# Moving x's transposes behind P times V, and splitting tile 1's normalisation between VectorE and GpSimd, in a five-phase attention kernel

## The reference

```
def _attn(xq, xc, Wq, Wk, Wv, Wo, bo):          # 16 heads of 64
    q, k, v = xq @ Wq, xc @ Wk, xc @ Wv
    attn = softmax(q k^T * 64 ** -0.5)
    return (attn v) @ Wo + bo
x = _attn(_ln(x, g1, b1), _ln(x, g1, b1), ...1) + x      # SELF
x = _attn(_ln(x, g2, b2), context, ...2) + x             # CROSS
x = _geglu_ff(_ln(x, g3, b3), Wp, bp, Wf, bf) + x        # GEGLU
out = attention of 16 heads of 8 over the context        # CROSS2
return x + out + ffn(_ln(out, ln_g, ln_b))               # FFN
```

## Time and profile before

| | |
|---|---|
| median of 3 runs | 451.22 us (450.65 to 452.02) |
| the profiled execution | 450.97 us, span 449.3 us |
| granted TensorE clock | 1.0 of full speed in all 40 slices |
| PE busy | 434.4 us, 97% of the span |
| PE weight loads | 399.4 us, 89% |
| DVE / ACT / POOL busy | 352.9 (79%) / 318.8 (71%) / 201.8 us (45%) |
| chain that ended last | PE 88%, DVE 6%, ACT 2%, issue 2% |

### The profile page before, as it was taken

One profiled execution on the slowest core, in us unless ns is written; L12 is line 12 of the kernel. 1 busy time (PEld: TensorE's weight loads), 2 busy tenths in 40 slices (PEclk: granted clock), 3 DMA queues, 4 the chain that ended last, 5 costly groups with the idle time before them and its releaser, 6 DMA issues.

```text
span 449.3 us, 17107 instructions
## 1 busy us (share of the span) xinstructions
PE 434.4 (97%) x7513; PEld 399.4 (89%) x7513; DVE 352.9 (79%) x649; ACT 318.8 (71%) x587; POOL 201.8 (45%) x226
## 2 busy tenths in 40 slices
PE   8999999999999999999999999999999999999897
PEld 7979999898999999989989899889999777778797
DVE  4888889688797887978978789896784788898471
ACT  5686676777778768787677776876546576777763
POOL 1883332555345634555352533523342232152782
PEclk9999999999999999999999999999999999999999
DMA  7202021110200000000000000000000000000011
GB/s 230 58 4 85 3 85 28 53 48 4 63 4 4 10 3 11 12 3 10 12 2 12 3 10 13 3 3 1 2 1 19 10 12 19 4 1 4 13 36 47
DMA packets 14623, 10.61 MB, mean 24 GB/s; under 512 B 5188, under 2 KB 13592, under 8 KB 14552
## 3 DMA queue, kind: packets, MB, share of 16 engines
q1 hardware_dynamic: 14120, 9.48, 7.3%
q10 hardware_dynamic: 432, 0.07, 0.1%
HBM read 8.50 MB, written 1.05 MB: 21 GB/s over the span
## 4 chain that ended last, share of the span: by engine, by line
PE 88%; DVE 6%; ACT 2%; issue 2%; POOL 1%; DMA 1%; POOLq 0%
PE stage L683 12%; PE stage L684 11%; PE stage L685 11%; PE scp L865 8%; PE scp L788 7%; PE scp L837 6%; PE scp L944 6%; PE out0p L885 4%; PE out0p L913 4%; PE out0p L887 3%; PE out0p L886 3%; PE stage L849 3%; PE scp L805 2%; DVE pr L1417 1%; PE stage L934 1%
## 5 line engine op out<-in xcount | busy, mean ns | idle before, releaser
L1734 POOL TENSOR_TENSOR pr<-pr,rc 128x1024 f32<-128x1024 f32 (+1 forms) x32 | 59.1, 1867 | 76.5 <-DVE rc L1447 76.4
L1165 ACT ACTIVATE pr<-pr 128x1024 f32<-128x1024 f32 x48 | 50.8, 1059 | 36.7 <-DVE pr L1417 30.1
L1672 POOL TENSOR_TENSOR rstd<-veps,neghalf 128x2 f32<-128x2 f32 x32 | 22.8, 714 | 70.8 <-DVE veps L1365 70.6
L1099 ACT ACTIVATE vt<-stage 64x512 f32<-64x512 f32 x83 | 49.2, 592 | 4.8 <-PE stage L685 1.2
L1461 DVE COPY vt<-stage 64x512 f32<-64x512 f32 x45 | 31.2, 694 | 21.8 <-PE stage L685 20.9
L1412 DVE TENSOR_REDUCE mx<-scp 128x16 f32<-128x1024 f32 x32 | 39.2, 1224 | 8.9 <-PE scp L788 8.5
L1099 ACT ACTIVATE ot_h<-scp 128x512 fp32r<-128x512 f32 x64 | 33.4, 600 | 13.3 <-PE scp L865 13.3
L1467 DVE TENSOR_TENSOR ot_r<-scp,ot_h 128x512 fp32r<-128x512 f32 x64 | 40.0, 683 | 2.3 <-ACT ot_h L1099 1.0
L1099 ACT ACTIVATE k_of_heads<-stage 128x512 f32<-128x512 f32 x62 | 36.9, 598 | 5.4
L1417 DVE TENSOR_TENSOR pr<-scp,mx 128x1024 f32<-128x1024 f32 x32 | 39.2, 1224 | 1.1
L1445 DVE TENSOR_REDUCE sm<-pr 128x16 f32<-128x1024 f32 x32 | 38.0, 1188 | 0.0
(11 more groups left out here) (266 smaller groups left out, 1398.8 us busy)
## 6 DMA issues: line engine op xcount, KB each, us to landing
ctx_in<-in_ctx_dram SPq DMA_DIRECT2D x16, 96.0 KB, 2.0
masked_k<-in_L_xattn_Wo_dram SPq DMA_DIRECT2D x2, 512.0 KB, 3.8
out_dram<-rows SPq DMA_DIRECT2D x8, 128.0 KB, 1.8
rows<-in_x_dram SPq DMA_DIRECT2D x1, 768.0 KB, 9.4
pr<-in_L_xattn_Wq_dram SPq DMA_DIRECT2D x1, 512.0 KB, 4.9
pr<-in_L_xattn_Wk_dram SPq DMA_DIRECT2D x1, 512.0 KB, 6.2
pt<-in_L_xattn_Wv_dram SPq DMA_DIRECT2D x1, 512.0 KB, 7.6
rows<-in_L_xattn_Wq_dram SPq DMA_DIRECT2D x1, 512.0 KB, 5.1
```

The source lines that it names most:

```text
L1099: return nc.scalar.activation(dst, s, ACT.Copy)
L1165: nc.scalar.activation(pr[t][:, :], pr[t][:, :], ACT.Exp, scale=scale[s.phase]).then_inc(exped, 1)
L1734: nc.gpsimd.tensor_tensor(p, p, rc[:, t, h:, None].to_broadcast([ROWS, H - h, N]), ALU.mult)\
```

## The change

PE's order has `x_step(two)` behind both P times V steps and before the values; ACT has `x_turned_step(two)` behind its four `ot_h` copies; `Counts` follows. Tile 1 of every group but SELF 0 is now shared: DVE multiplies its heads 0 to 7 right after its last sum, and POOL only heads 8 to 15. PE waits for DVE's part before the first four transposes of tile 1 and for POOL's before the other four. Tile 0 stays with POOL (but in CROSS 7, which is as before).

```diff
+def shares(s, t):
+    if s.phase not in (SELF, CROSS) or s.is_group(SELF, 0):
+        return False
+    return t == 1 or s.is_group(CROSS, GROUPS - 1)
...
-                self.x(two.phase, two.first)
                 for i in range(4):
                     self.use("av", p, g, i)
+                self.x(two.phase, two.first)
...
+            if shares(Step(p, g), t):
+                self.tick("probs_dve", (p, g, t))
...
-                last_group = s.is_group(CROSS, GROUPS - 1)
-                if not last_group:
+                shared = shares(s, t)
+                if not shared:
                     pe.wait_ge(probs, cnt.at("probs", s, t))
                 for c in range(2):
-                    if last_group and c == 0:
-                        pe.wait_ge(probs_dve, t + 1)
-                    elif last_group:
+                    if shared and c == 0:
+                        pe.wait_ge(probs_dve, cnt.at("probs_dve", s, t))
+                    elif shared:
                         pe.wait_ge(probs, cnt.at("probs", s, t))
...
-                    x_step(two, s)
                     turn_step(s, 1)
                     av_step(s, 0)
                     av_step(s, 1)
+                    x_step(two, s)
                     val_step(one, range(3), s)
...
-                    x_turned_step(two)
                     pt_step(s, 1)
                     av_step(s, 0)
                     av_step(s, 1)
+                    x_turned_step(two)
                     val_step(one, range(3))
...
                     sum_step(one, 1)
                     if two.phase != GEGLU:
+                        probs_step(one, 1)
+                    if two.phase != GEGLU:
                         val_step(one, (3,))
...
-                h = H // 2 if s.is_group(CROSS, GROUPS - 1) else 0
+                h = H // 2 if shares(s, t) else 0
```

## The result

The changed kernel takes 455.9 us (median of 4 runs, 454.79 to 456.93) against 451.05 for the kernel before (4 runs, 450.65 to 452.02): a ratio of 1.0107 [1.0084, 1.013], 4.85 us slower. The profiled execution is the fastest of the four: 454.79 us, span 452.7 against 449.3, the clock granted in full. So its trace shows 3.4 to 3.8 us of the loss. In the kernel after, lines of PE, ACT and DVE stand 8 further down than in the rows before (L683 is L691, L1118 is L1126, L1461 is L1469), POOL's 10.

The account below looks back on a forecast made before the run. PE, busy 97% of its span, was taken to bound the kernel. Late bank less switch gain (1.3 us in 8 groups, 0.55 in 5) plus 0.65 in two pinned groups made +2.5: 453.5, given as 453.6, range 450.4 to 456.0.

Parts of the forecast that it names:

- a bank's wait of which nothing is absorbed: Third value projection: its load's whole lateness counts, 0.33 and 0.28 per group; +4.3 us in all, 455.5.
- the second rival: DVE's multiply of tile 1 comes behind both POOL multiplies, delaying P times V 0.2 in 14 groups: 456.6 us, chance 0.10.
- PE bounds, and the split alone is worth nothing: PE's own work sets the time; sharing tile 1's multiply gains and costs nothing, and only allows the move.
- DVE between POOL's two: Tile 1's multiply: DVE goes ahead of POOL's second multiply, lasting about 1.1 (held, then 0.55), at no cost.
- The late bank: Third value projection waits for ACT's later copies: load late by 0.33 or 0.28, net +0.16 in 8 groups, +0.11 in 5.
- The gain at the switch: Behind P times V, transposes take away part of a 0.11 switch before the values: gain 0.05 in each of 15 groups.
- The two pinned groups: SELF 0 and CROSS 6: P times V already waits, so moved transposes cost 0.22 plus 0.11, +0.33 each, 0.65 in all.
- The sum: Whole kernel: 1.3 + 0.55 + 0.65 = +2.5 us against the profiled execution's 450.97, with nothing for PE's stops.
- a rival on the faster side: PE's unexplained stops in P times V of SELF 3 and CROSS 3 vanish and the wait is absorbed: 448.9 us, chance 0.12.
- its own sign of being wrong: Profile after: load not late, DVE wait for pt before P times V, or stops of about 1 us gone or more.
- the signs of being right: Third value projection's load idle 0.1 to 0.3 in 15 groups; context groups 0.1 to 0.2 longer; DVE's multiply about 1.1.

Follow-up runs that it names:

- e2: The kernel before with only tile 1's multiply shared, x's transposes staying between the turns: 451.39 us, ratio 1.0.
- e3: The changed kernel without the shared multiply: x's transposes moved behind P times V, tile 1 multiplied by POOL alone; 458.5 us, ratio 1.0174.
- e4: The changed kernel with x's and the context's transposes going into the output projection's free PSUM bank: 451.41 us, ratio 1.0005.
- e7: The changed kernel with ACT copying x in four pieces of 64 columns, to lengthen the copy: 467.05 us, ratio 1.0356.
- e1: The changed kernel measured once more, without an edit: 456.31 us, ratio 1.0112.
- e6: The changed kernel with x's transposes and copy put back between the turns in SELF 0 and CROSS 6 only: 455.5 us, ratio 1.0112.
- e5: The changed kernel with x's transposes between tile 1's turns and P times V, and ACT copying x before its ot_h copies: 451.89 us, ratio 1.0022.
- e9: The changed kernel with half the output projection put between the two scores steps in SELF 3, SELF 4 and CROSS 3: 454.3 us, ratio 1.0082.
- e8: e2's kernel with x's transposes between the P times V steps (SELF 3, CROSS 3) and half the output projection between SELF 4's scores steps: 450.82 us, ratio 0.999.
- e10: e4's kernel with half the output projection put between the two scores steps in SELF 4 alone: 450.9 us, ratio 1.0003.

## Why the prediction was right, and where its size was off

The time is 455.9 where 453.6 was forecast in a range of 450.4 to 456.0, and the side, slower, is the likelier one. The mechanism was right and accounts for 2.5 of the 4.85 us. That the range held is luck: its upper end stood for a bank's wait of which nothing is absorbed, and a little of the second rival, and neither came about; 455.9 is 0.1 inside it, and the repeat, 456.31, is outside. Point by point:

*PE bounds, and the split alone is worth nothing.* Right: e2 is 1.0 [0.9987, 1.0014], and e3 shows that the split is needed for the move (4.3 us of waits for POOL).

*DVE between POOL's two.* Right: 1.13 for "about 1.1", in all 14 groups. POOL's own half takes 1.49 and not 1.04, which the working left out and nobody waits for. The order of the two agrees with the Trainium skill, page "SBUF — State Buffer", section "Who interferes with whom", by which the one that was issued first goes first: DVE issues at 211.24, POOL's second multiply only at about 211.8.

*The late bank.* Right in mechanism and in size. In CROSS 2 the third projection's load comes 0.60 behind the one before it, for 0.23 in the kernel before: late by 0.37 for a forecast of 0.33. In SELF 4 it is 0.53 for 0.23, late by 0.30 for 0.28. The groups with context and without a stop are longer by 0.12 to 0.18 for a forecast of 0.16, SELF 1, 2 and 5 by 0.10, 0.07 and 0.16 for 0.11. The wait's own price, the groups of the change less those of e4, is 0.17 to 0.19 without context and 0.22 to 0.25 with it (0.31 in CROSS 4), for 0.16 and 0.21. e4 takes the wait away and the loss is gone; e7 makes it larger and pays one for one. The load waits in 14 groups and not in 15, and its idle time there is 0.2 to 0.4, not 0.1 to 0.3.

*The gain at the switch.* It was put at 0.05 between 0 and 0.11; e4, without the wait, shows 0.01 to 0.12 in 9 of the 10 groups that have no stop over 0.6 and aren't pinned. The tenth, CROSS 4, has 0.18, since the kernel before has its stop of 0.40 there. Right.

*The two pinned groups.* The sum was right, 0.32 and 0.36 for 0.33, but by other parts, so its size is luck. In SELF 0 P times V starts 28.35 and the first value load 30.58, 2.23 apart; before it was 28.46 and 30.58, 2.12 apart. x's transposes behind P times V so cost 0.11 and not 0.22 + 0.11. The rest is the same bank's wait as elsewhere, which the working had left out for these two. In CROSS 6, in the loads of the kernel after:

```profile
291.06 1.99 PEld L873 LDWEIGHTS scp<-pt,vt 64*64 64x64 f32 x128 [0.91 <-issue]
...
293.29 0.19 PEld L691 LDWEIGHTS stage<-wv_of1h,ctx_src1h 96*128 96x128 f32 x1
...
294.86 0.19 PEld L691 LDWEIGHTS stage<-wv_of1h,ctx_src1h 96*128 96x128 f32 x1 [0.34 <-ACT xT L1126]
```

0.17 more before the first value load (2.23 for 2.06), and 0.34 of idle time before the third projection. e4, without the wait, shows the first part by itself: 0.14 and 0.19.

*The sum.* The direct part is 2.5 us, as forecast. **The term that was mis-sized is the stops**, which the sum put at nothing. The prediction knew two of the four that the kernel before has, and had them only as a rival on the faster side, with an aside that the shift "can also bring such a stop to a group that has none: +1.0", and "the number of instructions ahead of each run changes by less than ten" as a reason for no change. Two groups did get one, and its own sign of being wrong, "the stops of about 1 us gone or more in number", came true beside the signs of being right.

Three figures tell what the stops cost. In e1's trace, of an execution with the median time, SELF 3 and CROSS 3 together are 2.2 us longer than the bank's wait makes them. Added up in each trace, the stops of the five with the bank's wait and no cut (after, e1, e3, e6, e7) are 4.4, 6.3, 5.4, 5.8 and 6.3 us, and of the four without it (before, e2, e4, e5) 3.3, 3.9, 3.9 and 3.9: 1.9 less on the average. And e9 prices the two new ones in the scores at 1.0 to 1.4 us, while the longer ones ahead of them still make SELF 3 and CROSS 3 0.8 us longer there. So 2.5 us are the bank's wait and the pinned groups, and some 2 us, the larger part of what is left of the 4.85, are stops.

Why the stops come in the scores now is argued, not shown. In the record of PE's instructions, waits and branches included, every one of these stops, in all profiles here, stands 193 or 194 records into a block of 256. The trace has some one 16 KB packet of an instruction queue per such block (58 for 60). The traffic of the DMA engines of the kernel after from 86 to 88 us, in 40 slices of 0.05 us, and that queue:

```profile
DMA  0000000000000000000000000000000000000009
...
q8 instruction: 1, 0.02, 4.2%
```

This packet starts in the last slice, at 87.95 to 88.00, and takes 4.2% of 16 x 2 us, 1.3 us, until 89.3. PE reaches the place in SELF 3's scores at 89.5 and stands until 90.72. In the kernel before the packet starts in the slice at 87.55 and takes 0.9, until 88.5; PE reaches the place at 90.21, 1.7 later, and goes on. Over the SELF and CROSS groups of the twelve profiles there are 48 stops at this place (more than 0.35 us from load to load). Every one ends 1.2 to 1.6 us after the end of the latest packet, and 2.2 to 3.0 after its start. A run of 64x64 matmuls takes its 128 loads and 128 matmuls in 2.0 us, less than that. So PE most likely waits there for its next instructions; no run changes the queue by itself. In the profiles with the bank's wait the scores of SELF 3 or CROSS 3 stop; in those without (before, e2, e4, e5 and e8) they stop little or not at all, and e4 has PE's matmuls in the same order as the change. That fits a wait that holds the queue, so that the next packet is asked for later. But P times V stops for 1.72 in e4 without any such wait, so this isn't the whole rule, and it stays open.

## What to carry to other kernels

A step that is moved on a saturated engine takes its copy along on another one: look at what that copy will stand behind, and at who is next on its buffer. Here the transposes cost nothing in their new place, and 0.3 to 0.4 us of lateness behind ScalarE's busiest stretch cost a wait in 14 groups; another free bank gave all of the loss back (e4), and a place ahead of that stretch all but 0.9 of the 4.85 us (e5). Where a profile has stops that nothing explains, count them in several executions, and give them a term with both signs in the sum.

## What the runs showed of the hardware that was not expected

PE stopped for 0.4 to 1.7 us 193 or 194 records into a block of 256 of its instructions, where fast 64x64 matmuls stand around that place or before it, and by a different amount in two executions of one kernel (4.4 and 6.3 us in sum). Each such stop ended 1.2 to 1.6 us after the end of a 16 KB packet of the instruction queue. Slower matmuls ahead of the place took such a stop away in the scores (e8, e9 and e10) and not in P times V (e8).

A GpSimd multiply of 128x512 took 1.49 us instead of 1.04 when VectorE's multiply came in ahead of it, while VectorE's took 1.13 for some 0.55 of work: both are lengthened, VectorE by waiting for the one before and GpSimd by waiting for VectorE.
